# A new opening for a one-core kernel of two routed feed-forward layers: staging, sort, high halves and normalisation rearranged

## What is computed

```python
x = x + xattn(layernorm(x), token_ids, ctx, ctx, ctx)   # 4 experts, chosen by token id
x = x + ffn(layernorm(x), router_w, wg, wu, wd)          # 8 experts, chosen by argmax of x @ router_w.T

# layer 1, expert e:   y = (silu(h @ ctx[e].T) * (h @ ctx[e].T)) @ ctx[e].T       (float32)
# layer 2, expert e:   y = bitlinear(relu(bitlinear(h, wg[e]))**2 * bitlinear(h, wu[e]), wd[e])
# bitlinear: weights rounded to -1, 0, 1 times their mean absolute value, activations to 8 bits per row
```

## Time and profile before

| | |
|---|---|
| median of three runs | 270.26 us |
| the profiled execution | 268.87 us, its span 267.1 us |
| PE busy | 236.2 us (88%) |
| DVE, ACT, POOL busy | 214.6, 213.3, 159.1 us |
| granted PE clock | 0.99 of full speed over the span |

### The profile page before, as it was taken

One profiled execution on the slowest core, in us unless ns is written; L12 is line 12 of the kernel. 1 busy time (PEld: TensorE's weight loads), 2 busy tenths in 40 slices (PEclk: granted clock), 3 DMA queues, 4 the chain that ended last, 5 costly groups with the idle time before them and its releaser, 6 DMA issues.

```text
span 267.1 us, 5815 instructions
## 1 busy us (share of the span) xinstructions
PE 236.2 (88%) x1423; PEld 172.9 (65%) x1423; DVE 214.6 (80%) x678; ACT 213.3 (80%) x324; POOL 159.1 (60%) x315
## 2 busy tenths in 40 slices
PE   2286779999999999999999999988699999999970
PEld 2134558788888888888888888866345455555530
DVE  5959897988878788788878787887579799989861
ACT  2888878698889788889888789865789889999950
POOL 4435015577777777776776765357725577647553
PEclk9999999999999999999999999999999999999997
DMA  5999359365655555875555654153266799411110
GB/s 214 429 395 310 123 189 405 107 218 209 236 199 182 153 197 202 320 276 178 177 187 196 230 214 181 46 161 120 80 210 241 234 264 299 160 38 68 62 39 0
DMA packets 13839, 51.72 MB, mean 194 GB/s; under 512 B 2862, under 2 KB 2862, under 8 KB 10224
## 3 DMA queue, kind: packets, MB, share of 16 engines
q1 hardware_dynamic: 8928, 37.91, 41.1%
q0 software_dynamic: 4880, 13.44, 14.3%
HBM read 40.49 MB, written 13.48 MB: 202 GB/s over the span
## 4 chain that ended last, share of the span: by engine, by line
PE 64%; DVE 13%; issue 7%; POOL 5%; DMA 5%; SPq 4%; ACT 1%; POOLq 0%; DVEq 0%
PE bank L1292 34%; PE bank L1393 14%; PE bank L1285 8%; PE bank L1365 5%; PE bank L1387 2%; DVE ctx_lo L826 2%; DMA x<-x_rows,gather 2%; DMA x_rows<-filler 1%; SPq L367 1%; SPq L368 1%; DMA late_rows<-x_rows 1%; POOL out_rows L529 1%; DVE stats L882 1%; DVE hT_lo L906 1%; POOL x L434 1%
## 5 line engine op out<-in xcount | busy, mean ns | idle before, releaser
L1393 PE MATMUL bank<-ternary,qT 128*128 x184 | 43.7, 379 | 2.0 <-ACT qT L644 1.3
L566 ACT ACTIVATE ternary<-staged 128x2048 bf16<-128x2048 f32 x22 | 42.0, 1910 | 1.2 <-DMA staged<-weight_chunks 1.2
L572 ACT ACTIVATE ternary<-staged,w_scale 128x1536 int16<-128x1536 f32 x22 | 34.5, 1566 | 2.7 <-DVE w_scale L838 2.7
L485 POOL DMA_INDIRECT x_rows<-row,store_at x19 | 23.8, 1253 | 15.7 <-DVE var_eps L890 6.8
L1393 PEld LDWEIGHTS bank<-ternary,qT 128*128 128x128 bf16 x184 | 17.8, 97 | 22.7 <-issue 6.5
L529 POOL DMA_INDIRECT out_rows<-late_rows x18 | 19.9, 1105 | 16.1 <-DVE late_rows L1138 14.3
L434 POOL DMA_INDIRECT x<-x_rows,gather x19 | 21.4, 1124 | 12.2 <-DVE row L932 6.0
L1393 PE MATMUL bank<-ternary,rT 128*128 x92 | 23.6, 379 | 1.3 <-ACT rT L664 0.8
L600 ACT ACTIVATE pT_hi<-bank 128x512 fp32r<-128x512 f32 x19 | 11.4, 599 | 15.6 <-PE bank L1285 13.9
L444 POOL TENSOR_TENSOR rstd<-var_eps,half_powers 128x1 f32<-128x1 f32 x19 | 12.5, 658 | 18.6 <-DVE var_eps L890 18.0
L1292 PE MATMUL bank<-ctx_hi,hT_hi 128*128 x76 | 22.3, 415 | 0.7 <-DVE hT_lo L906 0.6
(11 more groups left out here) (213 smaller groups left out, 655.2 us busy)
## 6 DMA issues: line engine op xcount, KB each, us to landing
staged<-weight_chunks SPq DMA_DIRECT2D x22, 1024.0 KB
late_rows<-x_rows SPq DMA_DIRECT2D x18, 260.0 KB, 3.5
ternary<-ctx_chunks SPq DMA_DIRECT2D x4, 1024.0 KB, 8.9
x_rows<-filler SPq DMA_DIRECT2D x9, 260.0 KB
ternary<-weight_chunks SPq DMA_DIRECT2D x2, 1024.0 KB, 5.6
staged<-x_rows SPq DMA_DIRECT2D x5, 260.0 KB, 3.0
x<-x_rows,gather POOLq DMA_INDIRECT x19, 3.7
x_rows<-row,store_at POOLq DMA_INDIRECT x19
```

What stands on the lines that cost most here:

```text
L485: pool.indirect_dma_start(x1_rows, bass.IndirectOffsetOnAxis(ap=store_at[b % ROWS][:, :], axis=0), row[b % ROWS][:, :], None, bounds_check ...
L566: nc.scalar.activation(ternary[:, m * K * D:(m + 1) * K * D], staged[i % 2][:, :], ACT.Abs, accum_out=abs_sum[:, 2 * i:2 * i + 1]).then_in ...
L572: nc.scalar.activation(ternary[:, m * K * D + DVE_COLS:(m + 1) * K * D].bitcast(I16), staged[i % 2][:, DVE_COLS:], ACT.Copy, scale=w_scale ...
L1393: last = pe.matmul(ps[:, :], left[:, k * P:(k + 1) * P], ternary[:, bass.ds(e * (3 * K * D) + (kind * K + k) * D, D)], start=(k == 0), sto ...
```

## The change

It touches the opening alone, and the arithmetic of layer 1's normalisation.

- **Loads.** Matrices 2 and 3 get buffers of their own (`staged_early`, in ternary matrices 8 to 11, not yet written) with semaphores of their own. SP issues context 0, matrix 0, context 1, matrix 1, then waits for `gathering`, which POOL raises behind its first gather, and issues context 2, matrix 2, context 3, matrix 3 with no other wait. Matrices 4 and 5 wait for matrices 0 and 1. The filler rows are stored after matrix 4.
- **Sort.** The rounding is left to the conversion of `place_block` to int32 (one DVE step less). The multiplication of `block_hot` goes to POOL, between its first and its second `row_hot` tile; POOL makes 3 tiles, DVE 13; PE takes POOL's three just ahead of its last matmul. `gather1` is read in one step instead of two, ahead of the tables of experts.
- **High halves** of contexts 2 and 3 go from ACT to POOL (`tensor_copy`), behind `inverse_deviation(0)` and `gather(3)`.
- **Low halves** are made in two halves of 1024 columns each, spread over DVE's opening.
- **Normalisation.** `h` is x - mean only and waits no more for `rstd1`; `rstd1` enters in silu (as its scale) and in the gate (as a factor).
- **Orders.** DVE's opening is rearranged; the cuts of matrices 0 to 3 move to ticks 5 to 8. ACT evicts `hT(0)` ahead of `scale_part(1)`. PE makes `sum_mean(0)` before it waits for the table of experts, does 4, 2, 3 filling matmuls (before 4, 8, 4), starts the first product when the high halves are there, and does `sum_mean(3)` after the second product of block 0.

```diff
@@ sync
-                if i >= 2:
-                    sp.wait_ge(dve_part, i - 1)
-                    sp.wait_ge(act_part, i - 1)
-                sp.dma_start(staged[i % 2][:, :], weights_in[ORDER[i]]).then_inc(staged_in[i % 2], 16)
+                if i in (2, 3):
+                    sp.dma_start(staged_of(i), weights_in[ORDER[i]]).then_inc(staged_early_in[i - 2], 16)
+                    return
+                if i >= 4:
+                    last = i - 4 if i < 6 else i - 2
+                    sp.wait_ge(dve_part, last + 1)
+                    sp.wait_ge(act_part, last + 1)
+                sp.dma_start(staged_of(i), weights_in[ORDER[i]]).then_inc(staged_in[i % 2], 16)
...
             load_weights(1)
+            sp.wait_ge(gathering, 1)
             load_context(2)
+            load_weights(2)
             load_context(3)
-            for i in range(2, len(ORDER)):
+            for i in range(3, len(ORDER)):
@@ gpsimd
                 pool.tensor_scalar(row_hot[:, t, :], iota16[:, :], place_row[:, t:t + 1], None, ALU.is_equal)\
                     .then_inc(pool_hot_ready, 1)
+                if t == 0:
+                    pool.wait_ge(flagged, 1)
+                    pool.tensor_tensor(block_hot, block_hot, token1[:, :, None].to_broadcast(wide), ALU.mult)\
+                        .then_inc(blocks_hot_ready, 1)
+            def high_halves(e):
+                pool.wait_ge(ctx_in_sem[e], 16)
+                pool.tensor_copy(ctx_hi[:, e * K * D:(e + 1) * K * D], ctx_raw[e]).then_inc(pool_hi_ready, 1)
...
             pool.memset(fence[:, :], 0.0).then_inc(gathering, 1)
             gather(1)
             inverse_deviation(0)
+            high_halves(2)
             gather(2)
             inverse_deviation(1)
             gather(3)
+            high_halves(3)
@@ scalar
+                act.wait_ge(rstd1_ready, b + 1)
                 if b >= 1:
                     act.wait_ge(pT_ready, b)
-                nc.scalar.activation(p[:, :], a_ps[b % 2][:, :], ACT.Silu).then_inc(sil_ready, 1)
+                nc.scalar.activation(p[:, :], a_ps[b % 2][:, :], ACT.Silu, scale=rstd1[b % 2][:, :])\
+                    .then_inc(sil_ready, 1)
...
             scale_part(0)
-            high_halves(2)
+            evict_hT(0)
             scale_part(1)
-            evict_hT(0)
-            high_halves(3)
             sum_abs(2)
             silu(0)
@@ vector
-            link(dve.tensor_scalar(place_block[:, :], place_block[:, :], MAGIC, MAGIC, ALU.add, ALU.subtract))
...
-            link(dve.tensor_scalar(pad1[:, :], table_ps, 0.0, None, ALU.is_equal))
-            link(dve.scalar_tensor_tensor(gather1[:, :], table_ps, -1.0, pad1[:, :], ALU.add, ALU.add))
-            dve.sem_inc(sorted1, 1)
+            dve.tensor_scalar(gather1[:, :], table_ps, -1.0, 0.0, ALU.add, ALU.max).then_inc(sorted1, 1)
...
-                dve.wait_ge(rstd1_ready, b + 1)
+                dve.wait_ge(moments_ready, b + 1)
                 if b >= 1:
                     dve.wait_ge(hT_ready, b)
-                dve.tensor_scalar(h[:, :], x[b % RING][:, :], moments[b % 2][:, 0:1], rstd1[b % 2][:, :],
-                                  ALU.subtract, ALU.mult).then_inc(h_ready, 1)
+                dve.tensor_scalar(h[:, :], x[b % RING][:, :], moments[b % 2][:, 0:1], None, ALU.subtract)\
+                    .then_inc(h_ready, 1)
...
-                dve.tensor_tensor(p[:, :], a_ps[b % 2][:, :], p[:, :], ALU.mult).then_inc(p_ready, 1)
+                dve.scalar_tensor_tensor(p[:, :], a_ps[b % 2][:, :], rstd1[b % 2][:, :], p[:, :],
+                                         ALU.mult, ALU.mult).then_inc(p_ready, 1)
```

More of the change, by code:

```diff
@@ L28 @@
 QMAX = 127.0
-MAGIC = 12582912.0
 CAP = N + P
@@ L226, in moe_program, with staged_of @@
         ctx_raw = [spare(16 + 2 * e, 2 * K * D, F32) for e in range(E1)]
+        staged_early = [spare(8, 2 * K * D, F32), spare(10, 2 * K * D, F32)]
+        def staged_of(i):
+            return staged_early[i - 2] if i in (2, 3) else staged[i % 2][:, :]
         assert EXTRA[1] == MATS - 2
@@ L272, in moe_program @@
         staged_in = [sem(f"staged_in{i}") for i in range(2)]
+        staged_early_in = [sem(f"staged_early_in{i}") for i in range(2)]
         abs_ready, mean_ready, w_mean_ready, w_scale_ready = (
@@ L564, in sum_abs @@
                     act.wait_ge(extra_part, SCALE_PIECES * len(EXTRA))
-                act.wait_ge(staged_in[i % 2], 16 * (i // 2 + 1))
-                nc.scalar.activation(ternary[:, m * K * D:(m + 1) * K * D], staged[i % 2][:, :], ACT.Abs,
+                if i in (2, 3):
+                    act.wait_ge(staged_early_in[i - 2], 16)
+                else:
+                    act.wait_ge(staged_in[i % 2], 16 * (i // 2 + (i < 2)))
+                nc.scalar.activation(ternary[:, m * K * D:(m + 1) * K * D], staged_of(i), ACT.Abs,
                                      accum_out=abs_sum[:, 2 * i:2 * i + 1]).then_inc(abs_ready, 1)
@@ L572, in scale_part @@
                 nc.scalar.activation(ternary[:, m * K * D + DVE_COLS:(m + 1) * K * D].bitcast(I16),
-                                     staged[i % 2][:, DVE_COLS:], ACT.Copy, scale=w_scale[:, m:m + 1])\
+                                     staged_of(i)[:, DVE_COLS:], ACT.Copy, scale=w_scale[:, m:m + 1])\
                     .then_inc(act_part, 1)
@@ L821, in _, with low_half @@
                               ALU.subtract).then_inc(centred, 1)
[L823 to L827, removed]
+            def low_half(e, part):
+                first = part * K * D // 2
+                cols = slice(e * K * D + first, e * K * D + first + K * D // 2)
+                if part == 0:
+                    dve.wait_ge(*((ctx_hi_ready, e + 1) if e < 2 else (pool_hi_ready, e - 1)))
+                ins = dve.tensor_tensor(ctx_lo[:, cols], ctx_raw[e][:, first:first + K * D // 2],
+                                        ctx_hi[:, cols].bitcast(F32), ALU.subtract)
+                if part == 1:
+                    ins.then_inc(ctx_lo_ready, 1)
             def mean_of(i):
@@ L888, in variance @@
                 dve.bn_aggr(moments[b % 2][:, :], stats[:, :]).then_inc(moments_ready, 1)
+            def variance(b):
+                if not 0 <= b < B1:
+                    return
                 dve.wait_ge(moments_ready, b + 1)
@@ L1144, in _ @@
             scale_of(0)
-            low_halves(0)
-            scale_part(0)
+            low_half(0, 0)
             moments_of(0)
+            aggregate(0)
+            normalise(0)
             variance(0)
@@ L1150, in _ @@
             scale_of(1)
-            normalise(0)
+            low_half(0, 1)
+            hT_rest(0)
             moments_of(1)
+            aggregate(1)
+            normalise(1)
             variance(1)
-            scale_part(1)
-            hT_rest(0)
-            normalise(1)
-            cut(0)
-            low_halves(1)
+            scale_part(0)
+            low_half(1, 0)
             gate(0)
             hT_rest(1)
+            low_half(1, 1)
+            pT_rest(0)
             mean_of(2)
@@ L1163, in _ @@
             moments_of(2)
+            aggregate(2)
+            normalise(2)
             variance(2)
-            pT_rest(0)
-            normalise(2)
+            scale_part(1)
             scale_part(2)
-            cut(1)
-            low_halves(2)
+            low_half(2, 0)
             gate(1)
+            hT_rest(2)
+            low_half(2, 1)
             mean_of(3)
@@ L1173, in _ @@
             moments_of(3)
-            hT_rest(2)
+            aggregate(3)
             variance(3)
             scale_part(3)
-            cut(2)
-            low_halves(3)
+            low_half(3, 0)
+            low_half(3, 1)
             early, factors = early_slots(), mean_products()
@@ L1216, in _ @@
                     pass
-                if t == 2:
-                    cut(3)
+                if 5 <= t < 9:
+                    cut(t - 5)
                 if t in EXTRA_TOTAL:
@@ L1268, in _ @@
             pe.matmul(router_ps, ones[:, :], router_sum[:, :], start=True, stop=True).then_inc(router_mean_ready, 1)
+            pe.wait_ge(blocks_hot_ready, 1)
             for i in range(TILES - POOL_TILES):
+                if i == TILES - POOL_TILES - 1:
+                    for t in range(POOL_TILES):
+                        pe.wait_ge(pool_hot_ready, t + 1)
+                        pe.matmul(bank[6][:, 0:B1], row_hot[:, t, :], block_hot[:, t, :], start=False, stop=False)
                 pe.wait_ge(hot_ready, i + 1)
@@ L1286, in transpose1, with product1 @@
                 return last
-            def product1(ps, hi, lo, e):
+            def product1(ps, hi, lo, e, first=False):
                 pairs = [(hi, ctx_hi), (hi, ctx_lo), (lo, ctx_hi)]
                 for n, (left, right) in enumerate(pairs):
+                    if first and n == 1:
+                        pe.wait_ge(ctx_lo_ready, 1)
+                    if first and n == 2:
+                        pe.wait_ge(hT_lo_ready, 1)
```

(2 more changed lines are left out.)

46 lines of the change are left out of this document (24 added, 22 removed).

## The result

The changed kernel takes 274.13 us (median of four runs, 273.24 to 275.24), the kernel before 270.28 beside it: **1.54% slower**, ratio 1.0154 with a 95% interval of 1.0121 to 1.0187. The forecast was 269.3, with a range that ended at 271.2. Its profiled execution is 274.16 us, span 272.4.

What follows compares the result with a forecast made beforehand. PE was taken as the limit from 51.33 us on, so the change was worth what it moved that run's start. Terms of -0.6 and -0.4 gave -1.0 us, 269.3 off the median; range 266.8 to 271.2.

Steps and rivals of the forecast that it cites:

- step 4: DVE's opening, gate 0 to matrix 3's reciprocal: 2.1 us given back, so block 2's first product starts 0.6 us earlier.
- step 5: The loop from block 2's to block 4's first product: 0.4 us of lost time go, deferred cuts cost nothing.
- A granted clock below 1.00: In the opening of the profile after: listed among the signs that the forecast was wrong, with no size given.
- step 6: POOL's copies of contexts 2 and 3: 2.1 us each, with DVE needing neither before 30.6.
- first rival: POOL's copy of context 3 locks out DVE's `low(1,1)`: 0.8 us more given back, 270.1 us; chance 0.18.
- Step 1: The sort in the opening: `gather1` read at 12.2, 0.55 us sooner, and the fence at 14.65.
- Step 2: Opening loads: first gather usable at about 17, some 2.5 us earlier; matrix 2 usable at 22.5.
- fourth rival: The first gather does not come sooner: silu of block 0 loses 1.0, total change 0.0 us; chance 0.03.
- Step 3: Block 0: product 0 done near 23.4, silu at 24.5 behind matrix 2's sum, gate at 25.2, 2.7 us earlier.
- The rival with slow copies: POOL's copies in the opening: at 6.7 us each, +2.5 to +3.5 us, 273 us; chance 0.10.
- The sum: Whole kernel: -0.6 for block 2's first product and -0.4 in the loop make -1.0 us, 269.3 off the median.

Runs made afterwards that it cites:

- the late copy: Changed kernel, but POOL's copy of context 3 waits for DVE's low(1,1), so the two never run together; 271.82 us, ratio 1.0068.
- experiment 4: Changed kernel with POOL's copy of context 3 held until after low(1,1), and filling matmuls in two idle stretches of PE; 268.99 us, ratio 0.9965.
- Experiment 7: Kernel of experiment 4 without SP's wait for the first gather ahead of the loads of contexts and matrices 2 and 3; 272.4 us, ratio 1.0092.
- experiment 9: Kernel before with only the normalisation's part of the change, in silu, `h` and the gate; 268.95 us, ratio 0.9943.
- experiment 2: Changed kernel with filling matmuls, 10 ahead of block 1's first product and 14 ahead of the sum of matrix 4's mean; 269.69 us, ratio 0.9969.

## Why the prediction was wrong

**The clock, step 4 into step 5.** This is the step that failed. The prediction put block 2's first product at 39.0 and let it run as in the earlier trace rows. Its own numbers had PE's list ahead of that product done earlier while the sum of matrix 4 stayed where it was, so they implied an idle piece of some 4 us (an estimate) where there had been 2.00; I priced the wait and not what a wait does to the clock. "A granted clock below 1.00" stands in its last paragraph as a sign of error, but had no price and no rival. The runs showed two products at the lower level in its place, behind idle pieces of 2.78 and 3.46 us (granted clock 0.59 and 0.52). Measured: 1.0 us for the spell at block 1's product and 3.4 us for the one at block 2's, by the medians.

**The lockout, step 6 and first rival.** The mechanism was named, with a chance of 0.18 and a price of 0.8 us. `low(1,1)` lost 1.5 us, and the late copy gave 2.3 us, since the delay had also lengthened an idle piece of PE. Once PE's idle pieces are filled it is worth 0.1 to 0.7 us, under the rival's price and not clear of noise. The overlap came as the rival said, so it should have been in the forecast, and with the clock beside it.

**Step 1, the sort**: read of `gather1` at 12.03 for 12.2. The multiplication took 0.69 us for 1.2, but DVE's tiles took 2.83 us for 13, 0.22 each for 0.18; why is not shown.

**Step 2, the loads**: block 0's rows at 17.02 for 17. Matrix 2 was usable at 23.1, not 22.5 (at 23.8 in the trace of experiment 4), so the price of the later loads was 0.6 to 1.3 us too low; the second gather moved beside it. That gather landed at 22.9, 8.14 us after its issue. It hid behind block 0's product. Experiment 7 shows that the wait is worth 3.4 us to this order of work. That is not the fourth rival's case: without the wait the first gather lands at 21.1, later than the 19.68 of the kernel before.

**Step 3, block 0**: gate 0 at 25.87 for 25.2. Silu followed ACT's sum of matrix 2, as said, but product 0 was done only then too, at 25.1 for 23.4: its first eight matmuls took 3.6 us (20.40 to 24.02), for 1.9 in the kernel before. This first slow product was not foreseen either.

**Step 4, DVE's list**: gate 0 to ACT's part of matrix 3 took 12.6 us for 10.1: 1.5 of it the lockout, about 0.5 ACT's wait for the slow product (0.52 us idle before silu 1), the last 0.5 open. In experiment 4 the stretch took 10.24 us (26.41 to 36.65), so apart from the two causes the step was right. Its first terms add up to +1.4, not +1.3.

**Step 5, the loop**: the deferred cuts, the scaled silu and the longer gate (0.75 us for 0.69) cost the run nothing, as said.

**Step 6**: a copy took 1.90 us for 2.1. The rival with slow copies fell at once (6.7 us for 2048 columns would be 3.3 ns a column, not 3.1).

**The sum.** With both causes taken out (experiment 4) the kernel stands 1.4 us under the kernel before by the medians and 0.9 by the ratio, where the sum said 1.0. That agreement is luck, for its trace does not show the opening that the sum describes:

```profile
26.41 0.75 DVE L948 SCALAR_TENSOR_TENSOR p<-bank,rstd,p 128x512 f32<-128x512 f32 x1 [0.55 <-ACT p L648]
...
40.42 1.17 PE L1340 MATMUL bank<-ctx_hi,hT_hi 128*128 x4
...
56.29 1.18 PE L1340 MATMUL bank<-ctx_hi,hT_hi 128*128 x4
```

Gate 0 comes at 26.41 for 25.2, behind the later matrix 2, so step 3's 2.7 us are 1.5. Block 2's first product starts at 40.42, where the forecast said 39.0 and the kernel before had 39.64, and block 4's at 56.29, 0.25 us later than before instead of 1.0 sooner. The 0.4 us of step 5 did come (15.87 us between the two for 16.40). So in this trace the change, freed of both causes, gains nothing in the opening; where the medians gain is open, as in experiment 9.

## What to carry to other kernels

Where a change moves work of TensorE forward but not what the next piece waits for, add up the idle time that opens in one place, and price the product behind it at the lower clock, as a risk even where the idle piece is short. A few filling matmuls in that place are the cheapest test of it, and here also the cure. A copy that moves to GpSimd is best laid where VectorE has no two-operand work from SBUF: here such a subtraction stood still until the copy was done.

## What the runs showed of the hardware

- At the first product of the kernel after, four matmuls took 2.21 us, the time of the lower level, while the granted clock of that window reads 1.00. The filling matmuls just ahead are slow as well (3 in 1.49 us, for 0.23 us each in experiment 2's second filling). So here the durations tell the level, and the clock row does not:

```profile
20.40 2.21 PE L1338 MATMUL bank<-ctx_hi,hT_hi 128*128 x4
```

```profile
20.40:23.40 3.00, 3.00 (x9) 2.40 (x8) 1.07 (x2) 1.61 (x2) 2.57 (x2) 1.00 1.03 431
```

- A gather issued beside queued 1 MB loads landed 8.14 us after its issue. In the kernel after, none of its bytes moved from 17 to 19 us, while context 2 came in; from 19 to 22 us they moved beside those of matrix 2. The queues' rows (packets, MB, share of 16 engines) of 17 to 19 us, then of 19 to 22:

```profile
q1 hardware_dynamic: 114, 0.86, 103.4%
...
q1 hardware_dynamic: 133, 0.99, 78.3%
q0 software_dynamic: 78, 0.26, 22.4%
```

- The time of a run goes with its granted clock. Of the runs of the kernel before in the first set, one took 268.56 us at 0.994, one 270.36 at 0.983, one 272.50 at 0.975. The traces show low spells in different places: in the opening, near 180 us, near 190 to 200 us. What decides whether one comes stayed open.
